# Self-attention: the softmax division moved from the head outputs to the probability rows

## The reference, cut to what matters

```python
wei = jnp.einsum('bhtd,bhsd->bhts', q, k) * scale
wei = jnp.where(causal[None, None], wei, NEG_INF)
wei = jnp.where(tgt_padding_mask[:, None, None, :], NEG_INF, wei)
wei = jax.nn.softmax(wei, axis=-1)
sa_out = _merge(jnp.einsum('bhts,bhsd->bhtd', wei, v)) @ sa_wproj + sa_bproj
```

## Time and profile before

| | |
|---|---|
| time, median of 3 runs | 1355.68 us (1355.58 to 1355.85) |
| the profiled execution's own time | 1353.37 us |
| its span, first to last instruction | 1351.3 us |
| mean granted TensorE clock | 0.993 |
| busy, share of the span | PE 96%, PEld 80%, DVE 58%, ACT 49%, POOL 52% |

### The profile page before, as it was taken

How to read it: one execution, slowest core, us unless ns; L and a number is a source line. 1 busy time by engine, 2 the same in 40 slices (tenths; PEclk the granted TensorE clock), 3 DMA queues, 4 the chain that set the end, 5 groups by cost and what they waited for, 6 DMA issues and landing times.

```text
span 1351.3 us, 24602 instructions
## 1 busy us (share of the span) xinstructions
PE 1299.2 (96%) x9193; PEld 1074.6 (80%) x9193; DVE 787.9 (58%) x2003; ACT 663.2 (49%) x1611; POOL 699.9 (52%) x582
## 2 busy tenths in 40 slices
PE   6999999999999999999898999999999999999997
PEld 6888888888878888888787787878778787887874
DVE  6712223223677777776655575756657575675575
ACT  5411111222666766566625456564655647456444
POOL 3233131323434664559653767675676756667661
PEclk9999999999999999999998999999999999999999
DMA  7400102113657575697577666768667577766641
GB/s 236 142 28 16 63 32 71 41 61 112 132 156 204 146 187 146 162 225 212 157 133 126 117 94 115 131 114 139 95 137 111 104 131 125 124 101 108 92 71 42
DMA packets 102128, 160.06 MB, mean 118 GB/s; under 512 B 10389, under 2 KB 63421, under 8 KB 100730
## 3 DMA queue, kind: packets, MB, share of 16 engines
q1 hardware_dynamic: 102010, 158.50, 55.8%
HBM read 70.93 MB, written 28.31 MB: 73 GB/s over the span
## 4 chain that ended last, share of the span: by engine, by line
PE 82%; POOL 6%; DVE 5%; issue 3%; ACT 2%; DMA 2%; SPq 0%; POOLq 0%; ACTq 0%; DVEq 0%
PE ps L1777 20%; PE ps L164 13%; PE ps L453 12%; PE ps L423 10%; PE ps_pair L1794 6%; PE ps L1809 6%; PE ps L1823 5%; PE ps L1886 3%; POOL ca_partial L1639 2%; POOL ca_xT L1518 2%; PE ps L1246 1%; PE ps L1266 1%; PE ps_pair L1236 1%; PE ps L1841 1%; DMA ca_k_stack<-ca_keys 1%
## 5 line engine op out<-in xcount | busy, mean ns | idle before, releaser
L1716 DVE TENSOR_REDUCE ca_maxes<-ps 112x1 f32<-112x375 f32 x512 | 256.9, 540 | 112.9 <-PE ps L1809 110.8
L1660 ACT ACTIVATE ca_probT<-ps_pair 125x448 f32<-125x448 f32 x384 | 210.3, 554 | 180.3 <-PE ps_pair L1794 178.4
L1639 POOL TENSOR_TENSOR ca_partial<-ca_partial,ca_probT 125x896 f32<-125x896 f32 x118 | 249.3, 2112 | 93.6 <-ACT ca_probT L1660 88.9
L312 POOL TENSOR_TENSOR ff_hT<-ff_hrelu,ff_hT 128x512 fp32r<-128x512 f32 (+1 forms) x64 | 78.8, 1233 | 203.3 <-DVE ff_hT L394 203.3
L1809 PE MATMUL ps<-ca_k_stack,ca_q_stack 96*112 96x376 f32 x512 | 167.8, 352 | 4.0 <-DVE ca_mrow L1744 2.1
L1794 PEld LDWEIGHTS ps_pair<-ca_q_stack,ca_k_stack 98*125 98x125 f32 x768 | 130.2, 186 | 44.0 <-issue 31.9
L1794 PE MATMUL ps_pair<-ca_q_stack,ca_k_stack 98*125 98x224 f32 x768 | 156.2, 285 | 1.3 <-ACT ca_probT L1660 1.2
L423 PE MATMUL ps<-ff_w,ff_hT 128*128 128x512 f32 x672 | 155.5, 390 | 0.0
L1777 PE MATMUL ps<-ca_xT,w_a 128*128 128x376 f32 x768 | 154.3, 337 | 0.2 <-issue 0.2
L1777 PE MATMUL ps<-w_b,ca_xT 128*125 128x512 f32 x576 | 151.6, 400 | 2.5 <-POOL ca_xT L1518 2.5
L423 PEld LDWEIGHTS ps<-ff_w,ff_hT 128*128 128x128 f32 x672 | 125.6, 188 | 25.8
(11 more groups left out here) (144 smaller groups left out, 2406.2 us busy)
## 6 DMA issues: line engine op xcount, KB each, us to landing
ca_k_stack<-ca_keys SPq DMA_DIRECT2D x96, 376.0 KB, 8.0
sa_Q_stack<-sa_rows SPq DMA_DIRECT2D x96, 112.0 KB, 3.6
sa_K_stack<-sa_rows SPq DMA_DIRECT2D x96, 112.0 KB, 3.7
ca_q_stack<-q_out SPq DMA_DIRECT2D x96, 112.0 KB, 9.4
ctx_tokens<-in_ctx_dram SPq DMA_DIRECT2D x14, 672.0 KB
ctx_tokens<-in_L_xattn_ff_w_dram SPq DMA_DIRECT2D x16, 512.0 KB, 4.4
q_out<-sa_yT SPq DMA_DIRECT2D x16, 448.0 KB, 4.1
wp_lo<-wp_out SPq DMA_DIRECT2D x6, 1024.0 KB, 4.8
```

Of the source, the lines that this page charges most:

```text
L312: pool.tensor_tensor(hT[:, LO, m % RING, 0:width(g)], hrelu[i % 2][:, 0:width(g)], hT[:, HI, m % RING, 0:width(g)].bitcast(F32), ALU.subtr ...
L1639: pool.tensor_tensor(total, total, half(a), ALU.add).then_inc(partial_done, 1)
L1660: act.activation(probT[u // GH][0:JT, u % GH].rearrange("p a t -> p (a t)"), ps_p[u % 2][0:JT, 0:2 * T], ACT.Exp).then_inc(exp_done, 1)
L1716: dve.tensor_reduce(maxes[:, q, j, a:a + 1], ps_s[n % 3][0:TQ, 0:JH], AX_X, ALU.max).then_inc(s_read, 1)
```

## The change: the row is divided before its transposes

The inverse of each head's sums is taken head by head (`recip n-1` in slot n, behind DVE's copy of head n-2), and the row of exponentials is multiplied by it in place, in SBUF, in two instructions per head (112x112 and 112x224, with the inverse as a per-partition scalar). Even heads are multiplied by VectorE right behind the inverse; odd heads by ScalarE, behind `exp n` of the next head. PE's transposes then wait for `even_divided` or `odd_divided` instead of `exp_done`. The tiles `rinv`, `rinv_T` and `of` go, with the two transposes per group, ACT's copy of the transposed inverses and DVE's product; ACT rounds the value product straight from PSUM and DVE takes the rest from PSUM, both one slot behind the value product. The value product waits for `olo_done` of the group two before instead of `of_done`.

```diff
@@ plan_self_attention
         if 0 <= n - LAG < 16 * B:
             items.append(("prob", n - LAG))
+        if 0 <= n - 1 < 16 * B:
+            items.append(("recip", n - 1))
         items += reads[n]
         if b < B:
             items.append(("exp", n))
-        if (n - LAG) % 4 == 2 and 0 <= n - LAG < 16 * B:
-            items.append(("recip", (n - LAG) // 4))
+        if 0 <= n - 1 < 16 * B:
+            items.append(("divide", n - 1))
         items += rests[n]
...
             items.append(("value", G))
-            reads[n + 1].append(("sums_read", G))
-            rests[n + 1].append(("scale", G))
-            reads[n + 2].append(("scale_hi", G))
-            rests[n + 2].append(("scale_lo", G))
+            reads[n + 1].append(("output_hi", G))
+            rests[n + 1].append(("output_lo", G))
@@ scalar
-                                     accum_out=sums[:, (n // GH) % 2, q, h % GH:h % GH + 1])
+                                     accum_out=sums[:, n % 4, q:q + 1])
             ins.then_inc(exp_done, 1)
-        if name == "sums_read":
+        if name == "divide" and item[1] % 2 == 1:
+            n = item[1]
+            act.wait_ge(inv_done, n + 1)
+            for q in range(2):
+                row = prob[:, n % 4, TQ * q:TQ + T * q]
+                ins = act.mul(row, row, inv[:, n % 4, q:q + 1])
+            ins.then_inc(odd_divided, 1)
+        if name == "output_hi":
             G = item[1]
             act.wait_ge(o_psum, G + 1)
-            act.copy(rinv_T[:, G % 2], ps_o[G % 2][:, T:2 * T]).then_inc(rinvT_done, 1)
...
-            act.copy(oT[:, HI, G % KT], of[:, G % 2]).then_inc(ohi_done, 1)
+            act.copy(oT[:, HI, G % KT], ps_o[G % 2][:, 0:T]).then_inc(ohi_done, 1)
@@ vector
         if name == "recip":
...
+            n = item[1]
+            dve.wait_ge(exp_done, n + 1)
+            dve.reciprocal(inv[:, n % 4], sums[:, n % 4]).then_inc(inv_done, 1)
+            if n % 2 == 0:
+                dve.wait_ge(inv_done, n + 1)
+                for q in range(2):
+                    row = prob[:, n % 4, TQ * q:TQ + T * q]
+                    ins = dve.tensor_scalar(row, row, inv[:, n % 4, q:q + 1], None, ALU.mult)
+                ins.then_inc(even_divided, 1)
+        if name == "output_lo":
             G = item[1]
             dve.wait_ge(ohi_done, G + 1)
-            dve.tensor_tensor(oT[:, LO, G % KT], of[:, G % 2], oT[:, HI, G % KT].bitcast(F32),
+            dve.tensor_tensor(oT[:, LO, G % KT], ps_o[G % 2][:, 0:T], oT[:, HI, G % KT].bitcast(F32),
                               ALU.subtract).then_inc(olo_done, 1)
@@ tensor
         if name == "prob":
             n = item[1]
-            pe.wait_ge(exp_done, n + 1)
+            pe.wait_ge(odd_divided if n % 2 else even_divided, n // 2 + 1)
...
             if G >= 2:
-                pe.wait_ge(of_done, G - 1)
+                pe.wait_ge(olo_done, G - 1)
...
-            pe.wait_ge(recip_done, G + 1)
-            for q in range(2):
-                pe.transpose(o[:, T + TQ * q:T + TQ * (q + 1)], rinv[:, G % 2, q, :], ident)
```

More of the change, by code:

```diff
@@ L840, in self_attention @@
     maxes = sb("maxes", [TQ, 4, 2], F32, 87296)
[L841 to L845, removed]
+    sums = sb("sums", [TQ, 4, 2], F32, 87328)
+    inv = sb("inv", [TQ, 4, 2], F32, 87392)
     oT = sb("oT", [P, 2, KT, T], F32R, 142336)
@@ L860, in self_attention @@
         sem(n) for n in ("causal_ready", "mask_ready", "mask_half", "masks_ready", "bias_added"))
[L861 to L864, removed]
+    s_psum, max_done, inv_done = (sem(n) for n in ("s_psum", "max_done", "inv_done"))
+    even_divided, odd_divided = sem("even_divided"), sem("odd_divided")
+    exp_done, t_psum, o_psum, probT_done = (
+        sem(n) for n in ("exp_done", "t_psum", "o_psum", "probT_done"))
+    ohi_done, olo_done = sem("ohi_done"), sem("olo_done")
     t_read, hi_done, thi_done = sem("t_read"), sem("hi_done"), sem("thi_done")
@@ L1068, in scalar @@
             n = item[1]
-            h = n % H
             act.wait_ge(max_done, n + 1)
@@ L1073, in scalar @@
                                      ACT.Exp, bias=maxes[:, n % 4, q:q + 1], scale=-1.0,
-                                     accum_out=sums[:, (n // GH) % 2, q, h % GH:h % GH + 1])
+                                     accum_out=sums[:, n % 4, q:q + 1])
             ins.then_inc(exp_done, 1)
-        if name == "sums_read":
+        if name == "divide" and item[1] % 2 == 1:
[6 more added lines that the diff above has]
+        if name == "output_hi":
             G = item[1]
             act.wait_ge(o_psum, G + 1)
-            act.copy(rinv_T[:, G % 2], ps_o[G % 2][:, T:2 * T]).then_inc(rinvT_done, 1)
-        if name == "scale_hi":
-            G = item[1]
-            act.wait_ge(of_done, G + 1)
             if G % KT == 0 and G > 0:
                 wait_psum(act, ("P", G // KT - 1, 1))
-            act.copy(oT[:, HI, G % KT], of[:, G % 2]).then_inc(ohi_done, 1)
+            act.copy(oT[:, HI, G % KT], ps_o[G % 2][:, 0:T]).then_inc(ohi_done, 1)
         if name == "round_y":
@@ L1299, in self_attention @@
                      "query_stacks": (stacked["Q"][KT - 1], STACKED * B), "key_stacks": (stacked["K"][KT - 1], STACKED * B), "maxima": (max_done, H * B), "probabilities": (probT_done, H * B),
-                     "scaled": (of_done, KT * B), "value_products": (o_psum, KT * B), "results": (fin_done, B),
+                     "scaled": (olo_done, KT * B), "value_products": (o_psum, KT * B), "results": (fin_done, B),
                      "results_stored": (res_stored, 16), "prepared_weights": (wo_stored, 32 * len(prepared)),
```

## The result

The changed kernel takes 1422.25 us (median of four runs, 1420.87 to 1425.76), against 1355.76 for the kernel before beside it: a ratio of 1.0493, 95% interval 1.0475 to 1.051. The direction was right, and the range held by 2 us (1371 to 1424); the forecast size, +39 us, was too small: +66.5 was measured.

The account below looks back on a forecast made before the run. PE, holding 82% of the chain of waits, was taken as the bound. 8 batches x (3.8 + 2.2) = 48, less 9, less 4, plus 4 gave +39 us: 1395 us, own range 1379 to 1410, eight in ten 1371 to 1424.

Parts of the forecast that it names:

- nine places: Self-attention slots where PE's transposes would wait for scalings: five on ACT, 3.8 us, and four on DVE, 2.2 us per batch.
- The odd path, 2.79 us: From the score load of head n+1, through its exp and ACT's scalings of head n, to PE's transposes: 2.79 us.
- The even path, 2.12 us: From one head's transposes, through DVE's copy, inverse and two scalings, to the next head's transposes: 2.12 us.
- I add 0.15 for the pair, as about half of the time POOL runs: Allowance of 0.15 us for POOL delaying an even head's two DVE scalings, on top of 0.50 us.
- Slot 0: Even head's transposes at the batch's turn, with DVE held by two splits and the prepared weights: 0.87 us of new waiting.
- PE's saving, 9 (6 to 12): Two transposes fewer in each of 32 groups, 0.28 us a pair: 9 us less on PE.
- Old waits, -4: PE's wait of about 0.5 us per batch for DVE's residual vanishes behind the new waits: -4 us (0 to -8).
- The clock, +4: Two or three more falls of PE's granted clock, 1.7 us lost in each: +4 us (0 to 14).
- faster: Rival, 5%: scalings are done before PE asks, leaving only the removed transposes and up to -4: 1342 us.
- the waits overlap: Rival, 8%: a wait on one head gives the next one room, so half the 48 us: 1371.
- The clock: Rival, 7%: the granted clock falls in every batch, 14 us instead of 4: 1405.
- DVE and POOL block each other: Rival, 10%: both DVE scalings mostly wait for POOL, 0.43 us each, in four slots per batch: 23 us, 1418.

Follow-up runs that it names:

- experiment 2: The changed kernel with one kind of scaling left out: 1378.76 us with ACT's scalings alone, 1410.27 us with DVE's alone.
- experiment 6: The changed kernel with idle transposes of the identity filling PE's waits in five slots: 1417.94 us, ratio 1.0465.

## Why the prediction came out too low

Its steps, one by one. A head's lateness is added up here from the weight loads in the timelines: how much later than 0.12 us behind the start of the load before it, where it stands when nothing holds it, the first transpose load starts. By the slot in which the transposes stand, us, mean of batches 1 to 6 (of 0 to 7); the last line is the whole stage, all slots:

| slot | scaled by | forecast | changed kernel | `finish` cut in four |
|---|---|---|---|---|
| 1 | ACT | 0.72 | 0.76 | 0.75 |
| 5 | ACT | 0.59 | 1.22 | 1.23 |
| 9 | ACT | 0.59 | 0.84 | 0.85 |
| 13 | ACT | 1.03 | 0.95 | 0.84 |
| 15 | ACT | 0.90 | 0.70 | 0.71 |
| 2 | DVE | 0.28 | 0.67 | 0.43 |
| 10 | DVE | 0.76 | 2.60 | 1.15 |
| 12 | DVE | 0.28 | 0.24 | 0.31 |
| 0 | DVE | 0.87 | 1.88 | 1.88 |
| sum | | 6.0 | 9.9 | 8.2 |
| whole stage | | 48 | 76.1 | 66.4 |

- *Where.* All nine places were right, and in batches 1 to 6 no tenth of any size appeared; the first and the last batch have others (slot 8 of the first 1.29, slot 14 of the last 1.12). Each kind of scaling made its own waits, as the prediction argued: with the other kind left out (experiment 2) PE waited 31.6 us for ACT's (27.3 in the changed kernel) and 41.2 for DVE's (32.2).
- *The odd path, 2.79 us.* Right: ACT's scalings took 376 and 469 ns (388 and 469 taken from the earlier trace rows), and the five places sum to 4.5 us against 3.8. Slot 5 makes the difference: in two of the six batches ACT copies 128x1024 numbers of the prepared weights there (L1100, 2.04 us, from 494.20 and 547.41), and exp 4 starts late behind it.
- *The even path, 2.12 us: the term of the sum that was mis-sized most.* The step "I add 0.15 for the pair, as about half of the time POOL runs" failed: by the groups above a pair took 0.44 more than with POOL idle (630 + 416 against 279 + 328 ns). The step treated meetings with POOL as chance and spread them evenly; in an order written out by hand they recur at the same place, `finish` with head 8 in six of the eight batches. The four places took 5.4 us in place of 2.2, and 1.8 of the 3.2 more is slot 10. The trace of the kernel before had it: DVE's normalisation, 0.56 us long in the earlier trace rows, took three times as long beside `finish`, and by the prediction's own times the scalings of head 88 ran from 568.6 to 569.1, across the start of that instruction. POOL's and DVE's rows of the kernel before:

```profile
568.76 2.39 POOL L1063 TENSOR_TENSOR sa_fin<-sa_res,sa_fin 112x1024 f32<-112x1024 f32 x1
```

```profile
569.76 1.68 DVE L105 TENSOR_SCALAR sa_rhat<-sa_res,sa_ln_mean_var,sa_ln_rstd 112x512 f32<-112x512 f32 x1
```

- *The rule weighed.* The scaling at 614.11 ended after the POOL instruction that ran when it began, and with that instruction cut it got in between the pieces. The Trainium skill, "SBUF — State Buffer", section "SBUF: two separate sides", says just this of the pair (the loser waits for the whole instruction), and the trace agrees: 2.74 us against 1.29. The short meetings go the same way. Of the 39 scalings of 112 columns that began while a POOL instruction ran, 30 ended 0.07 to 0.08 us behind the end of that instruction; five began 0.21 us or less before its end and took 278 to 281 ns, as with POOL idle, and four don't fit, three of them in the last batch. So a meeting costs here what is left of POOL's instruction, less some 0.2 us. Head 92 is an ordinary case, POOL's row and DVE's:

```profile
626.87 0.67 POOL L157 TENSOR_TENSOR sa_rows<-sa_f,sa_rows 128x224 fp32r<-128x224 f32 x1
```

```profile
627.13 0.73 DVE L1166 TENSOR_SCALAR sa_prob<-sa_prob,sa_inv 112x112 f32<-112x112 f32 x2
```

  The prediction had the rule name the scalings as losers. The rule by itself names whoever starts second; by the profile's starts the eight scalings that began 0.04 to 0.05 us ahead of a POOL instruction waited for it, too.
- *Slot 0.* 0.87 had been forecast with scalings of 0.57. In the batch shown above they took 1.10 beside a mask addition and a split of POOL, and PE waited 1.54.
- *PE's saving, 9 (6 to 12).* By the weight loads 6.7: the pair's loads and the gaps before them; the gap before the value product stayed at 0.28, so the doubtful half of the 0.38 was the value product's own.
- *Old waits, -4.* More went: 6.4 us before the products and 3.5 before the value products.
- *The clock, +4: the second term that was too small.* The stage had 7 us at 1.2 GHz before (334 x 0.01 x 2, by its granted clock of 0.99), now 48 in nine stretches. The loads inside the products take 7.8 us longer in all (203.6 against 195.8), and the whole is an estimated 12 (below), three times the term. Little of the slow time lies inside waits: in the low stretches the transposes are late by 7.5 of their 76 us. The prediction took 340 to 382 us for the stretch where PE was least busy; in 625 to 667 it was busy for 37.0 of 42 us, and the clock was 0.96 there, too.

The sum by what was measured: 76.1 - 3.8 (lateness before the change) - 6.7 - 6.4 - 3.5 + 7.8 = 63.5 of the 67.8 us by which the span grew. The rest, 4.3, lies in PE's other loads (scores, value products, the first cross-attention items); experiment 6 shortened these, too, so most of it is likely the clock. With all of it the clock comes to 12.1.

Of the rivals, *faster* and *the waits overlap* fell, though the second's mechanism is there: PE came 36.7 and 46.6 us later to the transposes for the halves alone and 71.9 for both. *The clock* came about in seven of the eight batches, with an estimated 12 us for the 14 that it had. *DVE and POOL block each other* gave the nearest time (1418), and its 23 us are near the 26 (8 x 3.2) by which DVE's four places exceeded the forecast. It was right for a part of its reason: it priced 0.43 for each scaling in four slots alike, and more than half of the excess is one long meeting in one slot; and with no scaling on DVE at all the time is the same. That the range held is part luck: its upper end was set for the clock and the blocking one by one, both came about, and old waits that went (10 us in place of 4) made room. The forecast's own range, 1379 to 1410, did not hold.

## What to carry to other kernels

Before moving work onto the path between two products, count the whole chain (maxima, exponential, inverse, scaling) against the lag of the software pipeline; if it does not fit, a wait appears in every slot that is too short for it. Here that was so whichever engine did the work: moving the even heads from one engine to the other gained 1.4 us, one more slot 49 and 62. Then check that whatever hangs on the pipeline's other end can bear the extra slot, as the kernel before could not. In a hand-written order, look up what the other engine runs at the very place where the new instruction lands; an average busy share says nothing of a meeting that recurs in every batch. And where waits are added to TensorE, look at the granted clock behind them: here it added an estimated 12 us to the 72 of the waits.

## What the runs showed of the hardware that was not expected

DVE's in-place scaling of 112 columns takes 277 ns with POOL idle and up to 2167 beside one long POOL instruction. It ended 0.07 to 0.08 us behind the POOL instruction that ran when it began in 30 of 39 cases, and a POOL instruction with 0.21 us or less to go cost it nothing. Cutting the long instruction into four costs POOL 0.48 us (2.83 against 2.35) and saves the kernel 16.

The low-clock stretches of the changed kernel's stage, 48 us, lie for the most part behind the waits and not in them, and at the lower level twelve weight loads take 2.64 us and not 1.42. Idle transposes in the waits halved the slow time: PE's way to the transposes grew by 9.7 us, all else shrank by 12.8, and the kernel gained 4.3.
